# Attention maxima of a fused GNN and FFN kernel: fewer transposes, and a row laid by DMA

## The reference

```python
def _attention(x, Wqkv, Wproj):
    B, T, D = x.shape
    qkv = (x @ Wqkv).reshape(B, T, 3, H, HD)
    q, k, v = (qkv[:, :, 0], qkv[:, :, 1], qkv[:, :, 2])
    scores = jnp.einsum('bqhd,bkhd->bhqk', q, k) * jnp.float32(HD) ** (-0.5)
    attn = jax.nn.softmax(scores, axis=-1)
    out = jnp.einsum('bhqk,bkhd->bqhd', attn, v).reshape(B, T, D)
    return out @ Wproj
```

## Time and profile before

| what | value |
|---|---|
| median of 3 runs | 1528.83 us (1528.14 to 1533.79) |
| the profiled execution | 1530.04 us |
| its span in the trace | 1528.3 us |
| PE busy | 1411.6 us, 92% of the span |
| DVE busy | 1153.9 us, 76% |
| ACT busy | 969.3 us, 63% |
| POOL busy | 492.4 us, 32% |
| mean granted clock of PE | 0.972 |

### The profile page before, as it was taken

How to read it: one execution, slowest core, us unless ns; L and a number is a source line. 1 busy time by engine, 2 the same in 40 slices (tenths; PEclk the granted TensorE clock), 3 DMA queues, 4 the chain that set the end, 5 groups by cost and what they waited for, 6 DMA issues and landing times.

```text
span 1528.3 us, 25668 instructions
## 1 busy us (share of the span) xinstructions
PE 1411.6 (92%) x8981; PEld 1336.4 (87%) x8981; DVE 1153.9 (76%) x1756; ACT 969.3 (63%) x1658; POOL 492.4 (32%) x366
## 2 busy tenths in 40 slices
PE   3998799999799999999999999999999998699996
PEld 1897577999699999899898998999988898599996
DVE  5788979735689762486877878778788787788885
ACT  7997787523368432366848767478587522599995
POOL 1000000000000010244625536256356501288886
PEclk9999799999899999999999999999999998799999
DMA  7001000122214540000000000000001496466652
GB/s 201 2 1 37 5 14 18 52 99 73 101 55 131 182 142 22 1 21 1 1 21 0 21 0 0 21 0 0 21 1 32 119 295 169 126 155 163 164 94 35
DMA packets 52312, 99.09 MB, mean 65 GB/s; under 512 B 10848, under 2 KB 26852, under 8 KB 52224
## 3 DMA queue, kind: packets, MB, share of 16 engines
q1 hardware_dynamic: 39769, 72.55, 15.4%
q0 software_dynamic: 11376, 22.29, 7.4%
q10 hardware_dynamic: 1079, 3.13, 0.7%
HBM read 67.15 MB, written 44.31 MB: 73 GB/s over the span
## 4 chain that ended last, share of the span: by engine, by line
PE 68%; DVE 9%; issue 3%; DMA 1%; ACT 1%; POOL 1%; POOLq 0%; SPq 0%; ACTq 0%; DVEq 0%
PE ps L372 14%; PE ps L373 14%; PE ps L374 14%; PE ps L823 4%; PE ps L864 4%; PE ps L843 3%; PE ps L866 3%; PE ps L845 3%; PE ps L865 3%; DVE mcol L1072 2%; PE ps L1257 1%; PE ps L598 1%; DVE prlo L1035 1%; PE ps L832 1%; PE ps L1669 1%
## 5 line engine op out<-in xcount | busy, mean ns | idle before, releaser
L1035 POOL TENSOR_TENSOR prlo<-prob,prhi 125x500 fp32r<-125x500 f32 x180 | 251.7, 1404 | 267.4 <-ACT prob L976 266.2
L1072 DVE TENSOR_REDUCE mcol<-ps 125x1 f32<-125x1250 f32 x120 | 174.9, 1458 | 72.6 <-PE ps L823 72.0
L974 ACT ACTIVATE prhi<-ps 125x500 fp32r<-125x500 f32 x300 | 176.9, 590 | 71.0 <-PE ps L845 64.9
L864 PE MATMUL ps<-prhi,vhi 125*128 125x250 f32 x600 | 172.2, 287 | 8.5 <-POOL prlo L1035 4.3
L976 ACT ACTIVATE prob<-ps 125x500 f32<-125x500 f32 x300 | 176.5, 588 | 0.6 <-DVE prlo L1035 0.6
L1524 POOL MEMSET q<- 128x2500 f32 x1 | 2.2, 2187 | 529.4 <-PE ps L374 529.4
L866 PE MATMUL ps<-prlo,vhi 125*128 125x250 f32 x600 | 168.6, 281 | 0.0
L865 PE MATMUL ps<-prhi,vlo 125*64 125x250 f32 x600 | 167.6, 279 | 0.0
L843 PE MATMUL ps<-qst,kst 128*125 128x250 f32 x600 | 155.9, 283 | 3.5 <-issue 1.4
L372 PE MATMUL ps<-hhi,pthi 125*125 125x384 f32 x400 | 153.6, 384 | 3.0 <-DVE ptlo L712 3.0
L1669 PE MATMUL ps<-ohs,ohd 128*125 128x417 bf16 x380 | 126.1, 384 | 32.4 <-DVE ohs L2112 29.6
(11 more groups left out here) (330 smaller groups left out, 4023.1 us busy)
## 6 DMA issues: line engine op xcount, KB each, us to landing
w1all<-in_L_ffn_W_dram SPq DMA_DIRECT2D x8, 1152.0 KB, 10.1
w2st<-in_L_ffn_W_dram SPq DMA_DIRECT2D x8, 1152.0 KB, 6.6
wqst<-in_L_ffn_Wqkv_dram SPq DMA_DIRECT2D x12, 384.0 KB, 4.2
hid_d<-tin SPq DMA_DIRECT2D x10, 375.0 KB
hin<-hid_d SPq DMA_DIRECT2D x10, 375.0 KB
vtin<-xn_d SPq DMA_DIRECT2D x10, 375.0 KB
out_dram<-accr POOLq DMA_DIRECT2D x10, 375.0 KB, 8.8
xres<-in_x_dram SPq DMA_DIRECT2D x10, 336.0 KB
```

Source lines behind the costliest of these rows:

```text
L864: pe.matmul(ps[:, b:b + GQ], vhi[:, e, kt, :], hi, start=kt == 0, stop=False)
L974: act.activation(prhi[:, n % RING, :], bank(3 + n % 3, P, 2 * GQ), ACT.Exp, scale=float(HD) ** -0.5)
L1035: eng.tensor_tensor(prlo[:, n % RING, :], prob[:, n % 3, :], prhi[:, n % RING, :].bitcast(f32), ALU.subtract)\
L1072: dve.tensor_reduce(mcol[:, e, t:t + 1], ps[0:P, 0:N], AX.X, ALU.max, negate=True).then_inc(sem("max"), 1)
```

## The change

For head 1 of a pair (in the code `e == 1`, whose list is `TURNED_M[0]`), one transpose turns all ten columns at once: 125 x 10 becomes 10 x 125 in PSUM. ACT copies that with one instruction into a new tile `mrow` in SBUF, and SP issues a DMA (`m_row`) that lays the ten rows of 125 behind one another into the row of `q2`. For head 0 (`TURNED_M[1] = (8, T)`), the first eight tiles are turned in that way behind unit 20, while the rough pass still has two tiles to go, and the last two go by two single transposes and one ACT copy of 1 x 250 behind unit 23 as before. All of them now use bank 0.

New waits come with it. PE's transpose behind unit 20 waits for eight reductions. PE's rough tile 8 of a head 0 waits for ACT's copy of the eight rows (`m_set`), because that bank is written again. ACT's copy into `mrow` waits for the DMA before (`m_in`). `start` waits for the DMA too. Ahead of the first pair the eight-tile transpose stands right behind rough tile 7, and ACT's copy stands between `v_out(8)` and `v_out(9)`. On SP, `m_row(p, 1)` and `m_row(p + 1, 0)` stand behind `load_qk(p + 1)` in each pair, and the last `m_row` behind the fourth of six loads of the projection's weights. The rest of the diff moves `gate` in memory, puts `mrow` over small tiles that are no longer needed, and gives two loads another semaphore.

```diff
+    mrow = put("mrow", [T, P], f32r, at=MROW)
...
-        MAXIMA_AT = (23, 23)
-        SET_M_AT = (23, 23)
+        MAXIMA_AT = ((23,), (20, 23))
+        TURNED_M = ((T,), (8, T))
...
                 else:
                     pe.wait_ge(sem("max"), 20 * p + 10 * e + t)
+                    if e == 0 and t == TURNED_M[1][0]:
+                        pe.wait_ge(sem("m_set"), 3 * p + 1)
...
-            def maxima(p, e):
-
-                pe.wait_ge(sem("max"), 20 * p + 10 * e + T)
-                for t in range(T):
-                    at = (t // 4) * BANK + t % 4 * P
-                    last = pe.transpose(ps[0:1, at:at + P], mcol[:, e, t:t + 1], ident[0:P, 0:P])
+            def maxima(p, e, i):
+
+                tiles = TURNED_M[1 - e][i]
+                pe.wait_ge(sem("max"), 20 * p + 10 * e + tiles)
+                if i == 0:
+                    last = pe.transpose(ps[0:tiles, 0:P], mcol[:, e, 0:tiles], ident[0:P, 0:P])
+                else:
+                    for t in range(TURNED_M[1 - e][0], T):
+                        at = (t - TURNED_M[1 - e][0]) * P
+                        last = pe.transpose(ps[0:1, at:at + P], mcol[:, e, t:t + 1], ident[0:P, 0:P])
                 last.then_inc(sem("m_raw"), 1)
...
-                pe.wait_ge(sem("m_set"), 4 * p + (2 * e + 2))
+                pe.wait_ge(sem("m_set"), 3 * p + (e + 2))
+                pe.wait_ge(sem("m_in"), 32 * p + (16 * e + 16))
...
             for t in range(T):
                 rough(0, 0, t)
+                if t == TURNED_M[1][0] - 1:
+                    maxima(0, 0, 0)
                 v_half(pe, (T + t) // 2, t % 2)
-            maxima(0, 0)
+            maxima(0, 0, 1)
...
-            def set_m(p, e):
+            def set_m(p, e, i):
                 r = 64 * (1 - e)
-                act.wait_ge(sem("m_raw"), 2 * p + e + 1)
-                act.activation(halves(q2[r:r + 1, e, 0:1000]), two(0, 1, 500), ACT.Copy).then_inc(sem("m_set"), 1)
-                act.activation(q2[r:r + 1, e, 1000:N], bank(2, 1, 250), ACT.Copy).then_inc(sem("m_set"), 1)
+                act.wait_ge(sem("m_raw"), 3 * p + (2 * e + i + 1))
+                if i == 0:
+                    if e == 1 or not isinstance(p, int) or p > 0:
+                        act.wait_ge(sem("m_in"), 32 * p + 16 * e)
+                    tiles = TURNED_M[1 - e][0]
+                    act.activation(mrow[0:tiles, :], bank(0, tiles, P), ACT.Copy).then_inc(sem("m_set"), 1)
+                else:
+                    at = P * TURNED_M[1 - e][0]
+                    act.activation(q2[r:r + 1, e, at:N], bank(0, 1, N - at), ACT.Copy).then_inc(sem("m_set"), 1)
...
             for t in range(T // 2, T):
+                if t == T - 1:
+                    set_m(0, 0, 0)
                 v_out(act, t)
-            set_m(0, 0)
+            set_m(0, 0, 1)
...
+            def m_row(p, e):
+                r = 64 * (1 - e)
+                tiles = TURNED_M[1 - e][0]
+                sp.wait_ge(sem("m_set"), 3 * p + (2 * e + 1))
+                sp.dma_start(q2[r:r + 1, e, 0:tiles * P].bitcast(f32).rearrange("o (t c) -> o t c", t=tiles),
+                             mrow[0:tiles, :].bitcast(f32)).then_inc(sem("m_in"), 16)
...
+            m_row(0, 0)
             with sp.Fori(0, H // 2 - 1) as p:
                 load_qk(p + 1)
+                m_row(p, 1)
+                m_row(p + 1, 0)
...
-            load_split_sp(sp, 3, wproj, wpst)
+            load_split_sp(sp, 3, wproj, wpst, range(4))
+            m_row(H // 2 - 1, 1)
+            load_split_sp(sp, 3, wproj, wpst, range(4, KD))
```

More of the change, by code:

```diff
@@ L141, in build @@
     zsum = put("zsum", [P, 2, 8], f32)
+    MROW = top[0]
     wsum = put("wsum", [P, T], f32)
     lnc = put("lnc", [P, T, 6], f32)
+    gate = put("gate", [P, T, NE], f32)
+    mrow = put("mrow", [T, P], f32r, at=MROW)
+    assert put.end <= top[0]
     mcol = put("mcol", [P, 2, T], f32)
     viol = put("viol", [128, 4], f32)
-    gate = put("gate", [P, T, NE], f32)
     FREE = top[0]
@@ L374, in three, with load_split_sp @@
             return pe.matmul(o, lhi, rlo, start=False, stop=stop)
-        def load_split_sp(sp, n, dram, stage):
-            for k in range(KD):
+        def load_split_sp(sp, n, dram, stage, chunks):
+            for k in chunks:
                 if k >= 2:
@@ L796, in project @@
                 if not isinstance(p, int):
-                    pe.wait_ge(sem("m_set"), 4 * p)
+                    pe.wait_ge(sem("m_set"), 3 * p)
                 for m in range(2):
@@ L818, in rough @@
                     if e == 1:
-                        pe.wait_ge(sem("m_set"), 4 * p + 2)
+                        pe.wait_ge(sem("m_set"), 3 * p + 2)
                 else:
                     pe.wait_ge(sem("max"), 20 * p + 10 * e + t)
+                    if e == 0 and t == TURNED_M[1][0]:
+                        pe.wait_ge(sem("m_set"), 3 * p + 1)
                 for c, (a, b) in enumerate(((0, 512), (512, 1024), (1024, N))):
@@ L884, in head @@
                         rough(*other, ROUGH_AT[e].index(j))
-                    if other is not None and j == MAXIMA_AT[e]:
-                        maxima(*other)
+                    if other is not None and j in MAXIMA_AT[e]:
+                        maxima(*other, MAXIMA_AT[e].index(j))
             def tail(p, e, js=range(UNITS - LAG, UNITS)):
@@ L981, in pair @@
             def pair(p, last):
-                steps = {SET_K_AT[0]: lambda: set_k(p, 1), SET_Q_AT: lambda: set_q(p, 1), SET_M_AT[0]: lambda: set_m(p, 1)}
+                steps = {SET_K_AT[0]: lambda: set_k(p, 1), SET_Q_AT: lambda: set_q(p, 1), MAXIMA_AT[0][0]: lambda: set_m(p, 1, 0)}
                 more = {}
@@ L986, in pair @@
                     more = {LAG - 1: lambda: set_raw(p + 1, (5,)), SET_K_AT[1]: lambda: set_k(p + 1, 0),
-                            SET_Q_AT: lambda: set_q(p + 1, 0), SET_M_AT[1]: lambda: set_m(p + 1, 0)}
+                            SET_Q_AT: lambda: set_q(p + 1, 0), MAXIMA_AT[1][0]: lambda: set_m(p + 1, 0, 0),
+                            MAXIMA_AT[1][1]: lambda: set_m(p + 1, 0, 1)}
                 else:
@@ L1431, in _ @@
             sp.wait_ge(sem("w_lo"), 4 * KD - 1)
-            sp.dma_start(row2[:, 0, :], bcast(ln2g)).then_inc(sem("row2_in"), 16)
+            sp.dma_start(row2[:, 0, :], bcast(ln2g)).then_inc(sem("lnrow_in"), 16)
             sp.wait_ge(sem("w_lo"), 4 * KD)
-            sp.dma_start(row2[:, 1, :], bcast(ln2b)).then_inc(sem("row2_in"), 16)
+            sp.dma_start(row2[:, 1, :], bcast(ln2b)).then_inc(sem("lnrow_in"), 16)
             leave(sp, "sync")
@@ L2329, in _ @@
             dve.tensor_tensor(wrhl[:, :, NE:2 * NE], wrst[:, :, :], wrhl[:, :, 0:NE].bitcast(f32), ALU.subtract).then_inc(sem("route_dve"), 1)
-            dve.wait_ge(sem("row2_in"), 32)
+            dve.wait_ge(sem("lnrow_in"), 64)
             for t in range(T):
```

## The result

| what | before | after |
|---|---|---|
| median | 1528.84 us (15 runs) | 1536.99 us (15 runs) |
| ratio | | 1.0048, 95% interval 1.0039 to 1.0056 |
| the profiled execution, its span | 1530.04, 1528.3 us | 1538.3, 1536.5 us |
| busy PE, DVE, ACT, POOL | 1411.6, 1153.9, 969.3, 492.4 us | 1404.9, 1146.5, 960.6, 498.4 us |

The changed kernel is slower by about 8 us, though PE, DVE and ACT are each busy for 7 to 9 us less. The forecast was 1527.6 us and its range ended at 1532.0, so it was wrong, and on the side of slower.

The account below looks back on a forecast made before the run. The prediction took PE as the bound, 68% of the last-ending chain, with DVE 9%. Terms -4.25 - 0.5 + 3.2 + 0.3 = -1.2 us gave a median of 1527.6 us, 8-in-10 range 1524.0 to 1532.0.

Parts of the forecast that it names:

- The prices: Turning the maxima: one transpose instead of ten saves 0.85 us; ACT's copy of 125 elements per row takes 0.24 us.
- Ahead of a projection: Head 1's turn, five times: PE runs without a wait, so 0.85 us per place comes through, -4.25 us in all.
- Ahead of the first pair: Head 0's early turn, once: PE waits for tile 7's reduction, then for ACT behind `v_out(8)`; together +3.2 us.
- The last pair: Head 1's start, once: PE waits for the row's DMA to land, 1.9 us for 5 KB; +0.3 us.
- At the end of a head 1: Head 0's turn, five times: unit 21 0.74 us late, unit 24 0.1 earlier, DVE and POOL's turns stay; -0.5 us in all.
- rival (a): DVE and POOL's turns change, or unit 20's wait is longer: +0.5 to +1.0 us at five places, 1530 to 1532.6; chance 0.15.
- (c): New stalls in the first or last pair bring another stretch at the lower PE clock, +1.6 us: 1529.2; chance 0.1.
- Rival (d): Head 0's row lands late by DMA, with 6.9 us available: about 1543 us; chance 0.04.
- What would show it: Profile signs, among them tile 7 to DVE's L1057 shorter by only 0.1 us; wrong if DVE's splits exceed 6.5 us together.

## Why the prediction was wrong

**The prices** of the transposes and copies were right: a single transpose instead of ten saved 0.88 to 0.99 us a place (forecast 0.85), and the copy of eight rows took 0.25 to 0.27 us (0.24).

**Ahead of a projection**: right in mechanism and size, -4.7 against -4.25. What was taken off was for a switch of shape, which cost nothing here: PE's next matmul begins 0.03 us behind the transpose.

```profile
774.31 0.27 PE L837 MATMUL ps<-ident,mcol 125*10 125x125 f32 x1
774.34 0.36 PE L852 MATMUL ps<-qst,kst 128*125 128x250 f32 x1
```

**Ahead of the first pair**: right, both waits and their size (+3.2), and that the shorter turn is worth nothing there since POOL's chain is late by the full amount.

**The last pair**: 0.0 instead of +0.3. PE went on 2.0 us after the issue of the row's DMA began, where the estimate was 1.9. The prediction's own terms, 1167.4 and 1.9, add up to 1169.3, which is no delay against 1169.32; what it put on top of them was not there:

```profile
1175.11 0.76 SPq L1441 DMA_DIRECT2D q<-mrow  x1
...
1177.12 0.35 PE L852 MATMUL ps<-qst,kst 128*125 128x250 f32 x1 [0.26 <-issue]
```

The row names no releaser; the row's DMA is the only wait of this start that the change has added. The Trainium skill's page "DMA: Bandwidth & Descriptors", section "Anatomy of one DMA — SWDGE (gpsimd) path", states about 2.0 us as the fixed cost of a DMA from GpSimd's queue. This one is from SP's, and 0.76 of its 2.0 us are the issue, so the two numbers lie close together without the one explaining the other.

**At the end of a head 1**: this is the step that failed, and it failed in one sentence, "DVE's second split begins behind the first, at 834.15 + 0.81 - 0.12 = 834.84, still before, so the turns stay". The stall of 0.74 us and its passing on undiminished were right. The 0.46 us of room between 834.84 and POOL's 835.3 was not there. In the times of the kernel before, so with the 0.10 us by which the traces differ added, DVE's second step asked at 835.22 and POOL at 835.21.
First and mainly, 0.38 us went because DVE's first step doesn't begin when unit 24's scores are there. Before, it did, after 0.54 us of idleness. But what DVE does ahead of it, a `prlo` and a copy of row sums, hangs on unit 23's exponentials, and is late by the whole 0.74 us, which is more than the 0.54. So the step begins at 834.27 in its trace, with no idleness before it, and not at 834.03. I moved the start of one instruction by the shift of its old releaser and did not ask which releaser comes last now.
Second, 0.09 us went on POOL's side. The prediction put its request "some 0.8 us earlier", but its own figures, 834.99 and 834.03, are 0.96 apart; measured it is 0.92. With 0.96, POOL asks at 835.17. DVE's first step, late by 0.74 less its 0.54 us of idleness, puts the second at 835.20. So the same sum, with these two steps put right, has POOL first.
The mechanism stood in the prediction as rival (a), with its 15% and at most 1.0 us a place. The order is decided by which request comes first, and both sides moved toward each other, DVE's later by 0.2 us and POOL's earlier by 0.9 us against the kernel before.

**Rival (a) was the right one, but under-priced.** The flipped order costs 1.0 us a place, the upper bound given there. What was missing is what follows: PE's wait grows to 1.9 us, and behind that the clock can fall, for 1.5 to 1.7 us more (1.9 to 2.1 us across such a place against 0.4). The clock stood as a rival of its own, (c), tied to the other stalls, for which it did not come true: the clock is granted in full from 624 to 640 us, around the waits of 1.55 and 1.14 us in the first pair, and the stretch at the lower level near 646 us was there before the change too (granted clock 0.55 from 644 us before, 0.54 from 646 us after). It came true for a wait that only (a) makes. Rival (d), the late row, had the sign of the result but not its cause.

**"What would show it"** held where it was to show the error: the splits took 0.81 + 2.57 + 1.77 + 1.86 = 7.0 us and not 6.5, and the distance from tile 7 to L1078 did not get shorter.

The exclusion itself: the step that starts 0.01 us behind POOL's instruction takes 2.57 us, 1.11 more than alone, and the one 0.07 us ahead takes 1.46. POOL's `prlo` takes 1.26 us when it is first here, as it does alone elsewhere in the trace, so it loses nothing by DVE's step beside it; 1.25 us of waiting and 1.32 of work make up the 2.57. These rows fit what the Trainium skill's page "SBUF — State Buffer", section "SBUF: two separate sides", states, an exclusive lock held for a whole instruction; of a port shared by halves one would expect that both are slowed.

## What to carry to other kernels

Where two engines take turns on something, look for the place where both ask within half a microsecond, and put a margin there first: a small instruction of the one that should come first, moved out of its way, was worth 9 us here, more than the 4.7 us that the change saved ahead of the projections. When a step is shifted, list all that it waits for and take the latest anew; an idle time in the profile is the slack against its old releaser alone. And price a flipped order with its consequence: here the wait that it makes was followed by a fall of the clock at 15 of the 20 places in these traces.

## What the hardware showed beyond that

- The order was decided the same way at all four places in each of the five traces in which it flipped, at distances of 0.01 to 0.03 us, and the other way in pair 0, at 0.05 to 0.07. Useless work on another engine (0.54 us of ACT, five times) made the kernel 7 us faster.
- The same wait of PE, 1.85 to 2.2 us, stands at 20 places, four in each of the five traces in which the order flipped. At 15 of them the shift grows by 1.9 to 2.1 us across it and at five by 0.4; the granted clock fell at the former and held at the latter. So such a wait has no fixed price: 1.0 us or 2.5. These counts are of one execution of each kernel, and no run here shows what decides between the two.
- A DMA of 4.9 KB within SBUF, from ten partitions to one, let PE go on 2.0 us after its issue began, 0.76 us of which was the issue, at the one place where PE came to wait for it; PE's idle time there was 0.26 us.
